# Sort products two table products behind, first table rows made while the edges load, and five of thirteen block ranks before the gathers

## What is computed

```python
xt = jnp.einsum('ni,rio->rno', x, weight)
messages = xt[edge_type, col]                     # col is dst
out = jax.ops.segment_sum(messages, row, num_segments=num_nodes)   # row is src
x = _layernorm(x + relu(out + bias))
```

## Time and profile before

| | us |
|---|---|
| median of 3 runs | 6104.6 |
| lowest, highest | 6097.33, 6129.88 |
| the profiled execution's own time | 6080.51 |
| its span, first to last instruction | 6078.8 |
| load stage, to DVE's first instruction of the next | 57.49 |
| table stage, to the first gather | 846.60 |

### The profile page before, as it was taken

How to read it: one execution, slowest core, us unless ns; L and a number is a source line. 1 busy time by engine, 2 the same in 40 slices (tenths; PEclk the granted TensorE clock), 3 DMA queues, 4 the chain that set the end, 5 groups by cost and what they waited for, 6 DMA issues and landing times. The chain is left out here.

```text
span 6078.8 us, 88190 instructions
## 1 busy us (share of the span) xinstructions
PE 4475.1 (74%) x19043; PEld 2954.8 (49%) x19043; DVE 4766.4 (78%) x15281; ACT 3289.2 (54%) x8847; POOL 3404.5 (56%) x3360
## 2 busy tenths in 40 slices
PE   5666667777777776655647888888888888886997
PEld 2222234444444444433435666666666666664555
DVE  7666569999999777644448999999999999996564
ACT  2444457778777777500215666666666666663222
POOL 1000037777777777776027777777777777770000
PEclk9999989999999999977879999999999999997999
DMA  4211223333333333335436666666666666663000
GB/s 132 82 67 63 67 80 106 106 106 106 106 105 106 106 106 106 105 106 97 139 96 196 194 193 192 192 194 194 192 193 193 196 194 195 193 191 90 1 14 29
DMA packets 349148, 778.95 MB, mean 128 GB/s; under 512 B 76927, under 2 KB 179926, under 8 KB 348628
## 3 DMA queue, kind: packets, MB, share of 16 engines
q0 software_dynamic: 214080, 658.04, 38.4%
q1 hardware_dynamic: 134548, 115.23, 6.0%
HBM read 691.39 MB, written 81.59 MB: 127 GB/s over the span
## 5 line engine op out<-in xcount | busy, mean ns | idle before, releaser
L1303 POOL DMA_INDIRECT big<-kv_table,walk_s x1664 | 1811.7, 1089 | 549.0 <-issue 483.4
L604 POOL DMA_INDIRECT big<-xt_table,big x1616 | 1534.6, 950 | 564.3 <-issue 535.1
L620 ACT ACTIVATE walk_s<-walk_s,big 128x128 bf16<-128x128 bf16 x4704 | 1468.1, 389 | 420.4 <-DVE walk_s L915 405.6
L780 PE MATMUL pb<-big,walk_s 128*128 128x256 f32 x3232 | 1029.4, 414 | 375.7 <-DVE walk_s L980 195.7
L1335 PE MATMUL pb<-big,early 128*128 128x264 f32 x3328 | 909.0, 420 | 288.9 <-ACT early L1389 208.3
L955 DVE TENSOR_TENSOR node_a<-node_a,pb 128x256 f32 x1616 | 664.0, 411 | 370.6 <-PE pb L780 362.1
L707 PE MATMUL pb<-walk_s 128*128 128x384 bf16 x1568 | 530.5, 338 | 489.0 <-ACT walk_s L620 456.0
L780 PEld LDWEIGHTS pb<-big,walk_s 128*128 128x128 f32 x3232 | 610.7, 205 | 537.8 <-DVE walk_s L980 270.0
L1335 PEld LDWEIGHTS pb<-big,early 128*128 128x128 f32 x3328 | 638.5, 201 | 445.8 <-ACT early L1389 237.6
L1323 PE MATMUL pb<-node_a,hot_t 128*128 x3328 | 838.7, 396 | 6.2 <-ACT hot_t L1378 3.4
L1375 ACT ACTIVATE early<-pb,neg_p 128x512 bf16<-128x512 f32 x416 | 285.8, 687 | 860.2 <-PE pb L1314 845.9
(11 more groups left out here) (274 smaller groups left out, 5622.1 us busy)
## 6 DMA issues: line engine op xcount, KB each, us to landing
xt_table<-big SPq DMA_DIRECT2D x98, 512.0 KB, 2.9
big<-kv_table,walk_s POOLq DMA_INDIRECT x1664, 3.7
big<-xt_table,big POOLq DMA_INDIRECT x1616
pens<-pen_table SPq DMA_DIRECT2D x832, 12.1 KB
kv_table<-big SPq DMA_DIRECT2D x49, 256.0 KB, 2.0
x_store<-big SPq DMA_DIRECT2D x49, 128.0 KB, 2.0
big<-in_x POOLq DMA_DIRECT2D x48, 128.0 KB, 2.3
big<-in_x SPq DMA_DIRECT2D x6, 1024.0 KB, 11.4
```

What stands on the lines that cost most here:

```text
L604: e.indirect_dma_start(sum_rows[:, q % SUM_ROWS, k, :], None, xt_table, bass.IndirectOffsetOnAxis(ap=idx_all[:, i:i + 1], axis=0))\
L620: ins = e.activation(hot_v[:, t % SORT_HOTS, v, :], hot_q[:, t % SORT_HOTS, :], ACT.Copy, scale=byte[:, t:t + 1])
L780: e.matmul(pb[:, SUM_AT + i % SUM_BANKS, 0:D], sum_hot[:, i % SUM_HOTS, :], sum_rows[:, q % SUM_ROWS, k, :], start=True, stop=True).then_i ...
L1303: e.indirect_dma_start(rows[:, q % ROW_RING, k, 0:2 * D], None, kv_table, bass.IndirectOffsetOnAxis(ap=src_i[:, i:i + 1], axis=0))\
```

## The change

- **Lag.** PE runs the slots of product n behind product n + 2 (`BEHIND = 2`). ACT still evicts product n and then weighs its slots.
- **Early rows.** `load_x`, `turn_x`, `keep_x`, `product`, `keep_product` and `store_xt` move to the load stage, and the first three node tiles (12 products, 6 stores) are made there: four products before the transposes of the edges, eight after. The weights and the bias are now loaded from ACT's queue, before ACT's share of the edge loads.
- **Load stage.** Only the last 128 columns of the arrays are padded, and the large loads no longer wait for that. POOL makes the record array (memset and three copies) instead of ACT. DVE makes the window array before it waits for the transposes. The record array and other scratch tiles lie in other SBUF arrays.
- **Ranks.** Block 0 alone is ranked before the slots. Blocks 1 to 4 are ranked between the 224 slots, one each 54 slots, with four counts or two scatter steps behind a slot. Blocks 5 to 12 follow in the gather stage, 160 slots apart, with four scatter steps in seven slots. The lags of the sealing steps grow (`collect` from 6 to 14, `carry_on` from 9 to 18).

```diff
+EARLY = 3
+RANK_FAST, RANK_SLOW = 54, 160
+TABLE_RANKS = 5
 assert T * P >= E and ITEMS % 4 == 0 and P < COLS <= 2 * P and BLOCKS > 8
-assert 6 * RANK_FAST <= PRE and PRE + (BLOCKS - 8) * RANK_SLOW < (BLOCKS - 1) * BT
+assert (TABLE_RANKS - 1) * RANK_FAST + 5 <= PRE and PRE + (BLOCKS - TABLE_RANKS) * RANK_SLOW < (BLOCKS - 1) * BT
...
+        def load_x(e, w):
+            if w == W - 1:
+                e.wait_ge(s_xz, 1)
+            if w >= 2:
+                e.wait_ge(s_xtr, w - 1)
+            e.dma_start(x_in[0:node_rows(w), x_slot(w), :], a["x"][w * P:w * P + node_rows(w), :])\
+                .then_inc(s_x[w % 2], 16)
+
+        def turn_x(e, w):
+            e.wait_ge(s_x[w % 2], 16 * (w // 2 + 1))
+            if w >= 1:
+                e.wait_ge(s_xtc, w)
+            for k in range(KC):
+                ins = e.transpose(pb[:, 5, k * P:(k + 1) * P], x_in[:, x_slot(w), k * P:(k + 1) * P], ident[:])
+            ins.then_inc(s_xtr, 1)
+
+        def keep_x(e, w):
+            e.wait_ge(s_xtr, w + 1)
+            if w >= 2:
+                e.wait_ge(s_xm, 4 * (w - 1))
+            e.activation(x_t[:, w % 2, :, :], pb[:, 5, 0:D].rearrange("p (k n) -> p k n", k=KC), ACT.Copy)\
+                .then_inc(s_xtc, 1)
+
+        def product(e, n):
+            w, half, q = n // 4, n // 2 % 2, n % 2
+            if n >= XT_BANKS:
+                e.wait_ge(s_xe, n - XT_BANKS + 1)
+            for k in range(KC):
+                ins = e.matmul(pb[:, XT_AT + n % XT_BANKS, :], x_t[:, w % 2, k, :],
+                               w0[:, k, half * 4 + q * 2:half * 4 + q * 2 + 2, :],
+                               start=(k == 0), stop=(k == KC - 1))
+            ins.then_inc(s_xm, 1)
+
+        def keep_product(e, n):
+            half = n // 2
+            e.wait_ge(s_xm, n + 1)
+            if n % 2 == 0 and half >= 2:
+                e.wait_ge(s_xst[half % 2], 16 * (half // 2))
+            e.activation(xt_out[:, half % 2, (n % 2) * 512:(n % 2 + 1) * 512],
+                         pb[:, XT_AT + n % XT_BANKS, :], ACT.Copy).then_inc(s_xe, 1)
+
+        def store_xt(e, n):
+            w, half = divmod(n, 2)
+            e.wait_ge(s_xe, 2 * (n + 1))
+            e.dma_start(xt_v[w * P:(w + 1) * P, half * 4:half * 4 + 4, :],
+                        xt_out[:, n % 2, :].rearrange("p (r o) -> p r o", r=4)).then_inc(s_xst[n % 2], 16)
+
...
         def load_edges(e):
+            load_whole(e, raw_i["src"], a["src"], s_rawload)
+            load_whole(e, raw_i["dst"], a["dst"], s_rawload)
+            load_whole(e, raw_i["type"], a["edge_type_8"], s_rawload)
             e.wait_ge(s_padded, 5)
-            for name, to in (("src", raw_i["src"]), ("dst", raw_i["dst"]),
-                             ("edge_type_8", raw_i["type"]), ("edge_weight1", raw_w)):
-                load_row(e, to, a[name], s_rawload)
-            load_row(e, raw_next, a["dst"][1:E], s_nextload)
+            load_rest(e, raw_i["src"], a["src"], s_rawload)
+            load_rest(e, raw_i["dst"], a["dst"], s_rawload)
+            load_rest(e, raw_i["type"], a["edge_type_8"], s_rawload)
+            store_xt(e, 0)
+            store_xt(e, 1)
             e.wait_ge(s_rec, 3)
...
+            for n in range(2, 2 * EARLY):
+                store_xt(e, n)
             e.wait_ge(s_recout, 32)
 
         def make_consts(e):
             c = Chain(e, s_gp0)
-            e.memset(rec, 0.0).then_inc(s_recz, 1)
+            load_x(e, 0)
+            load_x(e, 1)
...
+            c(e.memset(rec, 0.0))
+            e.wait_ge(s_rawload, 16 * 12)
+            e.wait_ge(s_float, 2)
+            for f, v in ((DST, raw_f["dst"]), (SRC, raw_f["src"]), (WGT, raw_w)):
+                e.tensor_copy(rec[:, :, :, f], v.rearrange("p (g e) -> p g e", e=P)).then_inc(s_rec, 1)
+            for w in range(2, EARLY + 2):
+                load_x(e, w)
 
         def edges_float(e):
-            e.memset(raw_i["src"], JUNK).then_inc(s_padded, 1)
-            e.memset(raw_i["dst"], JUNK).then_inc(s_padded, 1)
-            e.memset(raw_i["type"], 0).then_inc(s_padded, 1)
-            e.memset(raw_w, 0.0).then_inc(s_padded, 1)
-            e.memset(raw_next, JUNK).then_inc(s_padded, 1)
+            last = slice((RAW_G - 1) * P, RAW_G * P)
+            e.memset(raw_i["src"][:, last], JUNK).then_inc(s_padded, 1)
+            e.memset(raw_i["dst"][:, last], JUNK).then_inc(s_padded, 1)
+            e.memset(raw_i["type"][:, last], 0).then_inc(s_padded, 1)
+            e.memset(raw_w[:, last], 0.0).then_inc(s_padded, 1)
+            e.memset(raw_next[:, last], JUNK).then_inc(s_padded, 1)
...
             c(e.tensor_scalar(raw_i["src"], raw_i["src"], LOG_P, None, ALU.arith_shift_right))
             c(e.tensor_copy(win_b, raw_i["src"]))
+            e.wait_ge(s_badsum, 1)
+            c(e.tensor_scalar(unsorted[0:1, :], pb[0:1, 0, 0:1], 1.0, None, ALU.min))
+            e.wait_ge(s_cols, len(packs))
...
         def edges_turn(e):
             e.wait_ge(s_consts, 1)
+            turn_x(e, 0)
+            turn_x(e, 1)
+            e.wait_ge(s_w0, 16 * KC)
+            e.wait_ge(s_xtc, 1)
+            for n in range(4):
+                product(e, n)
             e.wait_ge(s_float, 3)
...
+            for w in range(1, EARLY):
+                if w + 1 < EARLY:
+                    turn_x(e, w + 1)
+                e.wait_ge(s_xtc, w + 1)
+                for n in range(4 * w, 4 * w + 4):
+                    product(e, n)
 
         def edges_cols(e):
...
-            e.wait_ge(s_recz, 1)
-            e.wait_ge(s_float, 3)
-            for f, v in ((DST, raw_f["dst"]), (SRC, raw_f["src"]), (WGT, raw_w)):
-                e.activation(rec[:, :, :, f], v.rearrange("p (g e) -> p g e", e=P), ACT.Copy).then_inc(s_rec, 1)
+            for k in range(KC):
+                e.dma_start(w0[:, k, :, :], a["L0_gnn_weight"][:, k * P:(k + 1) * P, :].rearrange("r p o -> p r o"))\
+                    .then_inc(s_w0, 16)
+            load_whole(e, raw_w, a["edge_weight1"], s_rawload)
+            load_whole(e, raw_next, a["dst"][1:E], s_nextload)
+            e.wait_ge(s_padded, 5)
+            load_rest(e, raw_w, a["edge_weight1"], s_rawload)
+            load_rest(e, raw_next, a["dst"][1:E], s_nextload)
+            e.dma_start(bias0, a["L0_gnn_bias"].rearrange("(a d) -> a d", a=1).to_broadcast([P, D]))\
+                .then_inc(s_bias0, 16)
+            keep_x(e, 0)
+            keep_x(e, 1)
+            for n in range(4):
+                keep_product(e, n)
...
+            for w in range(1, EARLY):
+                if w + 1 < EARLY:
+                    keep_x(e, w + 1)
+                for n in range(4 * w, 4 * w + 4):
+                    keep_product(e, n)
...
-        FIRST = 48
-        TABLE_RANKS = 8
+        SUM_BANKS, SUM_AT = 4, 2
+        FIRST, BEHIND = 48, 2
...
-            if t < PRE:
-                b, s = divmod(t, RANK_FAST)
-                return (2 + b, s, True) if 2 + b < TABLE_RANKS else (None, 0, True)
-            b, s = divmod(t - PRE, RANK_SLOW)
-            return (TABLE_RANKS + b, s, False) if TABLE_RANKS + b < BLOCKS else (None, 0, False)
+            for b in range(1, BLOCKS):
+                fast = b < TABLE_RANKS
+                s = t - ((b - 1) * RANK_FAST if fast else PRE + (b - TABLE_RANKS) * RANK_SLOW)
+                if 0 <= s < (RANK_FAST + 6 if fast else RANK_SLOW):
+                    yield b, s, fast
...
+            for n in range(2 * EARLY, 2 * W):
+                store_xt(e, n)
 
         def l0_gather(e):
...
+            for w in range(EARLY + 2, W):
+                load_x(e, w)
...
-                b = sealing(t, 1)
+                b = sealing(t, 3 if t < PRE else 1)
                 if b is not None:
                     keep(b)
-                b = sealing(t, 12)
+                b = sealing(t, 20)
                 if b is not None and b < BLOCKS - 1:
...
+            keep_x(e, EARLY)
             e.wait_ge(s_bias0, 16)
-            for w in range(W):
+            for w in range(EARLY, W):
...
+                    keep_x(e, w + 1)
                 e.activation(acc_w[:, w, 0:D], bias0, ACT.Copy).then_inc(s_acc0, 1)
                 for n in range(4 * w, 4 * w + 4):
...
+                    keep_product(e, n)
                     for t in slots_after(n):
                         slot(t)
+            for w in range(EARLY):
+                e.activation(acc_w[:, w, 0:D], bias0, ACT.Copy).then_inc(s_acc0, 1)
...
-                b = sealing(t, 9)
+                b = sealing(t, 18)
                 if b is not None and b < BLOCKS - 1:
                     carry_on(b)
-                b, s, fast = ranking(t)
-                if b is not None:
-                    if s == (7 if fast else W + 1):
+                for b, s, fast in ranking(t):
+                    if s == (13 if fast else W):
                         counts(b)
-                    if s == (12 if fast else W + 7):
+                    if s == (23 if fast else W + 8):
```

(96 more changed lines are left out.)

92 lines of the change are left out of this document (14 added, 78 removed).

## The result

| us | before | after |
|---|---|---|
| median of 4 runs each, measured in turn on one chip | 6117.24 | 5732.02 |
| lowest, highest | 6097.33, 6136.67 | 5728.48, 5733.86 |
| profiled execution | 6080.51 | 5733.86 |
| start of the stage behind the load stage | 57.49 | 69.09 |
| first sort | 185.4 | 142.87 |

The ratio is 0.937 (95% interval 0.9334 to 0.9406), 385 us less. The forecast was 5741, with the first gather at 484.8.

The account below looks back on a forecast made before the run. It took the table-stage chain of product, eviction, weighing and sort as the bound. 52 + 68.4 + 343 + 17 + 4.4 = 484.8 us to the first gather; with the rest unchanged and the runs' 1.004, 5741, range 5695 to 5830.

Parts of the forecast that it names:

- load stage: Start of the kernel: loads, edge transposes and eight early products were to end at 52 us, range 47 to 58.
- up to the first slot: After the load stage: PE makes products 12 to 49 and small products, 68 us, while DVE ranks block 0.
- slots, work of PE: In the 224 slots: 146 products 259 us, 224 sorts 76, small products and one seal 8; 343 in all.
- slots, DVE's stalls and the clock: In the slots: DVE falling behind in four ranks costs 12 us, PE's clock short of full 5 more.
- behind it: From the first gather to the end: left as in the kernel before, 5232.2 us, despite three more ranks there.
- Covered by PE's 47: Load stage: records ready by 34 us and stored by 44, hidden because PE's products last until 47.
- the 4 us named: Load stage: sum about 4 us longer if the shared port put off DVE's casts by up to 9.5 us.
- A: Rival, slots: DVE sets the pace of the fast ranks, 70 us for 12, total 5799; chance 10%.
- B: Rival, gather stage: DVE paces gathers in scatter parts, up to 94 us over eight ranks, total 5835; chance 10%.
- C: Rival, slots: the lag frees nothing, the 661 us stay, only the early part gains 62, total 6042; chance 3%.
- D: Rival, gather stage: DVE's rank operations hold up gathers, slower than before; 6190 at 0.35 us an item; chance 1%.
- The sign named for it: Sign, gather stage: POOL still at 80 to 81 gathers in 100 us at all times.

Follow-up runs that it names:

- e3: The changed kernel with POOL loading x tiles 2 and 3 ahead of its three record copies; 6461.74 us, ratio 0.943 to the kernel before.
- e7: The changed kernel with x loaded first, two ACT evictions ahead of its last edge loads, and POOL issuing the record store; 6554.01 us, ratio 0.9459.
- e9: The changed kernel with x tiles 2 and 3 loaded first and the three record copies on ACT instead of POOL; 5729.37 us, ratio 0.9362.
- e10: As e9, with the third and fourth product stores issued ahead of the record store; 5728.05 us, ratio 0.936.
- e1: The kernel before the change with only the lag added, slots of product n behind product n + 2; 6624.9 us, ratio 0.9676.
- e2: The changed kernel without the lag (`BEHIND` 0, the table stage's `sealing` lag back to 1); 6821.32 us, ratio 0.9947 to the kernel before.
- e5: The changed kernel run again, unaltered, in a group with slower gathers; 6559.3 us, ratio 0.9479 to the kernel before.
- e4: The changed kernel with gather-stage scatter steps one each second slot, not four in seven, and slow ranks 163 slots apart; 6487.5 us, ratio 0.9469.
- e11: The changed kernel run again, unaltered, beside e9 and e10; 5734.98 us, ratio 0.9369 to the kernel before.

## Why the prediction held, and where it did not

The first gather came within 0.4 us of the forecast, and the whole within 9. Both are errors that cancel:

| us | predicted | measured | |
|---|---|---|---|
| load stage | 52 | 69.1 | +17.1 |
| up to the first slot | 68.4 | 73.8 | +5.4 |
| slots, work of PE | 343 | 336.8 | -6.2 |
| slots, DVE's stalls and the clock | 17 | 0 | -17 |
| last eviction to the first gather | 4.4 | 4.7 | +0.3 |
| behind it | 5232.2 | 5247.7 | +15.5 |
| from the profiled execution to the median | +22 | -2 | -24 |

The last row is luck too. The span of the sum was 15 us too short. The forecast then added 0.4%, 22 us, because the median before lay that far above the profiled run. The four runs of the changed kernel lie within 5.4 us, and the profiled one is the slowest of them.

**The load stage** was mis-sized, and by more than its own range (47 to 58). The data were there at 24.05 (22 taken) and the columns at 35.7 (33): small. The step that failed is "POOL issues five loads of x, so the next stage finds tile 3 there". The first of them, tile 2, is needed within this stage, and POOL issues it behind the copies. It was counted as work for the next stage and not as a queue that PE waits in. The copies themselves were taken at 9.5 us, the upper bound, and took 13.3. In order, the 17.1 us are 1.8 until PE has the edges transposed (34.8 for 33), 11.6 of standing for tile 2, 2.4 for the eight products and 1.2 for the last eviction, its store and the barrier. The 2.4 are mostly clock: 32 matmuls took 16.1 us, for 14.1 by the earlier trace rows, and the stage's mean clock was 0.90.

e3 puts the order right and gets 7.1 of the 17.1 us back. e3, e7 and e9 show the next limit below it: the eight products need stores, and the record store of 3 MB is in their way. e10 takes them out of it, and then the record store is itself the limit. It ends no earlier than 57 us when its data come at 47. "Covered by PE's 47" held only because PE was late. One thing was left as it is in every run: four of the eight products, those of tile 1, need nothing of tile 2, which was late. They stand behind its transposes only because PE's program turns tile 2 first. At 7.1 us for four products they could fill a part of the 11.5; what that gives is not shown.

**The shared port.** The Trainium skill ("SBUF — State Buffer", section "SBUF: two separate sides") was quoted with the warning that the copies on POOL hold DVE's work up. It came about: three operations of 1.89, 1.03 and 1.03 us took 4.71, 1.96 and 3.83, 6.6 us more, and e9 shows that they do so only beside POOL. The hold goes both ways, as the changed kernel's trace shows. POOL's three copies, and DVE's operations of 1.03 to 1.89 us beside them, of which two stand above already:

```profile
26.19 4.68 POOL L473 COPY walk_s<-node_a 128x1664 f32<-128x1664 f32 x1 [13.70 <-DVE node_a L486]
30.72 4.86 POOL L473 COPY walk_s<-node_a 128x1664 f32<-128x1664 f32 x1
35.43 4.02 POOL L473 COPY walk_s<-node_a 128x1664 f32<-128x1664 f32 x1
...
25.93 1.88 DVE L488 SCALAR_TENSOR_TENSOR node_a<-node_a 128x1664 f32<-128x1664 int32 x1
...
32.48 1.89 DVE L495 TENSOR_REDUCE big<-big 128x1 f32<-128x1664 f32 x1
34.51 1.96 DVE L498 TENSOR_SCALAR node_a<-node_a 128x1664 int32<-128x1664 int32 x1
```

The three stretched operations end at 32.44, 36.47 and 40.33, each 0.9 to 1.6 us behind the end of a copy (30.88, 35.58, 39.45), a little less than their own length. The copies end 3.0 to 3.1 us behind the end of the DVE operation that was under way when they began (27.81, 32.44, 36.47). The reduction keeps its 1.89 us beside the second copy. So by these rows (an estimate) a copy that nothing holds up takes 3.1 us and the three 9.2, within the 9.5 taken. The other 4 us of the 13.3 are DVE's hold on POOL. The prediction priced POOL's hold on DVE and not this one. By the rule DVE's end was to move by up to 9.5 us; it moved by 4.9 between e9 and the changed kernel. It did not cost the 4 us named, since PE was later still.

**Up to the first slot** the sum counted one product too few (slot 0 stands behind product 50, 1.8 us), and 16 matmuls after the barrier took 9.3 us for 7.0, in part at the lower clock. PE also stood 0.6 us for ACT between the first two transposes.

**The slots.** The mechanism was right. e1 and e2 show it from both sides: without the lag PE waits 256 us, with it 82 (six ranks) or 4.7 (four). The work was put 6.2 us too high. A product was counted too many, a sort was taken at 0.34 for 0.33, and the small products at 8 for 6. The stalls of DVE, 12 us, did not occur: DVE is busy 286 of 342 us and waits 39 for PE. PE stands 4.7 us for weights in all. The lead that the ring and the lag give DVE is enough in each scatter part. The clock was 1.00, so the 5 us fell away too. Had the stage kept the 0.96 of before, some 14 us more would show, by the recorded sum (357 for 343).

**The rivals.** A (DVE paces the fast ranks) is refuted in this kernel, and e1 shows it alive where six ranks stand beside the slots. B (DVE paces the gathers) in its full size, 94 us, is refuted. But its place was right: the loss is in the scatter parts alone and is 12 to 17 us, where the forecast said none. Most of it lies in the gather instruction itself, though, which is D's way and not B's. C (the lag frees nothing) is refuted by e1 and e2. D (POOL's gathers held up by DVE's rank operations, from 0.28 us an item) is seen at 0.011 to 0.017 us a gather, a twentieth of the point from which it decides. The saying "the rows with and without a rank show no such delay" was read from counts of 80 and 81 in 100 us, and these can't show 1%. The sign named for it, 80 to 81 in every 100 us, did not hold either: the starts fall to 77 in one stretch.

**Behind the first gather** 12.2 of the 15.5 us are the gathers. The other 3.3 were not followed up.

## What to carry to other kernels

Where engines pass work in a ring, let the one that should be full run far enough behind its supplier; then look at once who is next, since here the lag alone gave 200 us, and the rest of the change, by e1's waits the thinned ranks above all, another 118 in the slots. A wait that is short but comes in each step costs twice, once as idle time and once as clock. In a stage that is refilled, write down for every queue which instruction of this same stage needs what is issued last.

## What was not expected of the hardware

- A copy of 128 x 1664 f32 with stride on POOL beside DVE took 4.0, 4.7 and 4.9 us, 2.4 to 2.9 ns an element. By the working above 3.1 of it are the copy and the rest is the hold of a DVE operation; no run has the copy on POOL alone. ACT takes 3.2 for it, and 3.4 in e9.
- Issuing a load can hold its engine long when others are queued ahead: 1.3 us for the two weight loads on ACT's queue together, then 3.7, 6.8 and 6.0 for the next three. Its first eviction starts at 21.30, though PE had transposed the first x at 8.7. The hold is waiting and not work: in e7 ACT evicts two tiles first and starts the second of these issues at 9.84 in place of 5.88. It then takes 3.0 us in place of 6.8 and ends at the same time, 12.8 for 12.7.
- A 512 KB store issued just behind a 3 MB store or beside it takes 9.5 to 10.4 us to land in place of 2.9, whichever engine issued the large one. ACT's evictions stood 6.9 to 11.7 us for it in e3, e7 and e9.
- Groups of runs differ in the pace of indirect gathers, 1.25 us or 1.54 to 1.62 within the ranks, with the same kernel and the same time up to the first gather. In e5 three gathers in four still come some 1.25 us apart; the others stand for PE (342 us in all) and for what the profile calls remote (199). Whether it is the chip is not shown: the record gives the same chip number to e1 to e4, which are slow, and to e9 to e11, which are not.
